# One LayerNorm statistics group instead of two, and another TensorE mark, at the entry of the first FFN

## The chip, the cores and the metric

One Trainium2 chip with 8 cores. Each core runs the same program on its own sequence (batch 8, one sequence of 2048 x 1024 for each core); no core waits for another. The time is in device microseconds of the slowest core.

## The reference

Four sublayers, each behind a LayerNorm and with a residual: a Mamba block, a gated FFN, causal attention, and the same FFN again.

```python
x = x + mamba(layernorm(x), W_in, conv_w, W_x, W_dt, b_dt, W_Bp, D_param, W_out)
x = x + ffn(layernorm(x), w_gate, w_up, w_down)
x = x + attn(layernorm(x), W)
x = x + ffn(layernorm(x), w_gate, w_up, w_down)

def ffn(x, w_gate, w_up, w_down):        # weights are int32 of -127..127
    gate = x @ (w_gate / 127).T          # 1024 -> 3072
    up   = x @ (w_up   / 127).T
    return (silu(gate) * up) @ (w_down / 127).T
```

## The kernel before

The instructions of each engine stand in the order in which the program text issues them (`em.op`); waits are on counting semaphores, and a mark such as `s_pe.mark()` is the count that a semaphore has reached at that point of the text.

**Mamba** works through the 2048 rows in 8 chunks of 256 (k = 0 to 7), each in 8 pairs. In the last chunk the FFN's gate weights are loaded beside it as int32 on SP's DMA queue and cast to bf16 by GpSimd, 16 units of 128 x 1536 (`emit_w_unit`, L803 to L826; SyncE issues the load, GpSimd casts, three staging slots in turn). `mamba_tail(7)` ends the block: VectorE adds the first half (L751), TensorE does 32 matmuls (L764), whose end is the mark `mk_t1[7]`, which is also `mk_mamba_pe_end`; VectorE waits for it and adds the second half (L774, `mk_mamba_ve_end`), and ScalarE's queue writes the sum to DRAM. GpSimd's last Mamba operation is `mk_mamba_gp_end`.

**The first FFN** (`ffn`, L871) has 4 chunks of 512 rows. Its first chunk finds its four input tiles in SBUF already, preloaded by `emit_ffn1_preamble`. `f_ln_tiles(c, tts, col0)` normalises some of them: `ln_stats_group` (L263) squares each tile on ScalarE (L269), sums it on VectorE (L278), does three small VectorE operations (L282, L284, L286), one square root on ScalarE (L291) and two or three small ones on VectorE. Then, tile by tile, VectorE normalises (L311), TensorE transposes 8 blocks (L322) and VectorE evacuates (L332). The first normalisation waits for a list of marks (L926 to L928).

What follows in the text, for the first FFN alone: 16 more units of `emit_w_unit`, which load and cast the up weights; then, on **ScalarE's queue**, 8 DMAs that write the cast gate weights to a bf16 copy in DRAM (`wg_c`, 768 KB each) and 8 that do so with the up weights (`wu_c`), each waiting for its casts (L952 to L960). The copies are read again by the last FFN. Then the first chunk's gate phase: 24 blocks of 8 matmuls (L993) into two PSUM banks in turn, each followed by a Silu on ScalarE (L1003), which frees the bank; then 24 blocks with the up weights, then the down projection (L1097). As the Silus stand behind the 16 cache DMAs in ScalarE's order, the first of them can't start before the last of those DMAs has been issued.

Of the kernel before, what the change touches and what calls it, by code (L numbers as in the profile page):

```python
# [26 lines left out]
NKM = L // TCM  # L27
# [130 lines left out]
def build_nc():  # L158
# [29 lines left out]
    with ExitStack() as ctx:  # L188
# [60 lines left out]
        s_pe = Sem(ctx.enter_context(nc.semaphore("s_pe")))  # L249
# [139 lines left out]
        def mamba_transpose(k, mk_free):  # L389
            par = k % 2  # L390
            banks = [4, 5]
            for tt in range(NTM):
                mk_tr = transpose_tile(xnbf[tt][:], banks[tt],
                                       mk_ln[k][tt], mk_free[tt])
                trdone[("m", tt)] = mk_tr
                mk_xnt[k] = evac_xnt(xnt[par], 256, tt, banks[tt], mk_tr)
# [183 lines left out]
        def phaseA_z_pair(kk, zp):  # L580
            par = kk % 2
            bkx = zp % 2
            for half in range(2):
                ci = NCI + 2 * zp + half
                wait_mm = [mk_xnt[kk], xzbank[bkx] if half == 0 else None]
                for dj in range(ND):
                    em.op("tensor",
                          lambda e, dj=dj, ci=ci, bkx=bkx, half=half, par=par: e.matmul(  # L588
                              psb[bkx][:, half * TCM:(half + 1) * TCM],
                              win_bf[:, dj * 4096 + ci * P: dj * 4096 + (ci + 1) * P],  # L590
                              xnt[par][:, dj * 256:(dj + 1) * 256],
                              start=(dj == 0), stop=(dj == ND - 1)),
                          wait=(wait_mm if dj == 0 else ()),
                          inc=([(s_pe, 1)] if (dj == ND - 1 and half == 1) else ()))
            mk_mm = s_pe.mark()
            w_sil = [mk_mm]
            if kk >= 1:
                w_sil.append(mk_gp_hist.get((kk - 1, zp)))
            elif zp == 0:
                w_sil.append(mk_startup)  # L600
            em.op("scalar",
                  lambda e, zp=zp, bkx=bkx: e.activation(
                      sz_bf[:, 2 * zp * TCM: 2 * (zp + 1) * TCM],
                      psb[bkx], AF.Silu),
                  wait=w_sil, inc=[(s_se, 1)], drain=False)
            xzbank[bkx] = mk_sz[(kk, zp)] = s_se.mark()
# [32 lines left out]
        def wout_t0(k, pi):  # L639
            w0 = [mk_gp_hist[(k, pi)]]  # L640
            if pi == 0:
                w0.append(mk_c67[0])
            for j in range(2):
                ci = 2 * pi + j
                for half in range(2):
                    em.op("tensor",
                          lambda e, ci=ci, half=half, bk=6 + half: e.matmul(  # L647
                              psb[bk],
                              y_bf[:, ci * TCM: ci * TCM + P],
                              wout_bf[:, ci * 1024 + half * 512: ci * 1024 + (half + 1) * 512],  # L650
                              start=(ci == 0), stop=(ci == NCI - 1)),
                          wait=(w0 if (j == 0 and half == 0) else ()),
                          inc=([(s_pe, 1)] if (j == 1 and half == 1) else ()))
# [149 lines left out]
        def emit_w_unit(gi):  # L803
            m2, r = divmod(gi, 16)
            dj, hh = divmod(r, 2)
            slot = (r % 2) if m2 == 0 else (r % 3)
            srcw = wg_t if m2 == 0 else wu_t
            dstw = wg_bf_g if m2 == 0 else wu_bf_g
            w = [mk_xz_last]
            if slot == 2:  # L810
                w.append(mk_mamba_pe_end)
            if w_prev[slot]:
                w.append(w_prev[slot])
            mkd = dma("sync", wstg[slot][:],
                      srcw[dj * P:(dj + 1) * P, hh * 1536:(hh + 1) * 1536],
                      wsem[slot], wait=w)
            cw = [mkd]
            if m2 == 1 and r == 0:
                cw += [mk_mamba_pe_end, mk_mamba_ve_end, mk_mamba_sta,
                       mk_mamba_stb]  # L820
            em.op("gpsimd",
                  lambda e, dj=dj, hh=hh, dstw=dstw, slot=slot: e.tensor_copy(
                      dstw[:, dj * H + hh * 1536: dj * H + (hh + 1) * 1536],
                      wstg[slot][:]),
                  wait=cw, inc=[(s_gp, 1)], drain=False)
            w_prev[slot] = w_mk[gi] = s_gp.mark()  # L826
# [17 lines left out]
        for k in range(NKM):  # L844
            for pi in range(8):
                phaseB_pair(k, pi)
                if k + 1 < NKM:
                    phaseA_xc_pair(k + 1, pi)
                    phaseA_z_pair(k + 1, pi)
                if k == NKM - 1 and N_SUBLAYERS >= 2:  # L850
                    emit_w_unit(2 * pi)
                    emit_w_unit(2 * pi + 1)
            if k + 1 == NKM - 1:
                mk_xz_last = s_pe.mark()
            wout_t0(k, 7)
            mamba_tail(k)
            if k + 1 < NKM:
                xp_sec(k + 1)
                if k + 2 < NKM:
                    mamba_load_ln(k + 2)  # L860
                    mamba_transpose(k + 2, [mk_xpe_k[k + 1], mk_xpe_k[k + 1]])
            if k == NKM - 2 and N_SUBLAYERS >= 2:
                ffn1_pre.update(emit_ffn1_preamble())

        mk_mamba_pe_end = s_pe.mark()
        mk_mamba_ve_end = s_ve.mark()
        mk_mamba_gp_end = s_gp.mark()
# [3 lines left out]
        def ffn(src, dst, first, region, store_mark_fn, pre=None):  # L871
# [6 lines left out]
            def fxt(c, tt):  # L878
                if pre and c == 0 and tt >= 2:
                    return fxB[tt - 2]  # L880
                if c % 2 == 1 and tt < 2:
                    return fxB[tt]
                return fxA[tt]
# [15 lines left out]
            def f_ln_tiles(c, tts, col0):  # L899
                tiles = [fxt(c, tt) for tt in tts]  # L900
                if pre and c == 0:
                    mk_x = pre["mk_loads"]
                else:
                    for i, tt in enumerate(tts):
                        gtile = c * NTF + tt
                        w = list(store_mark_fn(gtile))
                        if tt < 2:
                            if c <= 1:
                                w += region["xin"]
                            else:  # L910
                                w.append(mk_fst_chunk[c - 2])
                            if first and c == 1:
                                w.append(mk_fst_chunk[0])
                        else:
                            if c == 0:
                                w += region["xin"]
                            else:
                                w.append(mk_fst_chunk[c - 1])
                        mk_x = dma("scalar", tiles[i][:],
                                   src[gtile * P:(gtile + 1) * P, :],  # L920
                                   sd_x[c % 2], wait=w)
                mst = ln_stats_group([t[:] for t in tiles], col0, [mk_x])
                for i, tt in enumerate(tts):
                    col = col0 + i
                    ew = trdone.get(("f", tt % 2))
                    if pre and c == 0 and i == 0 and tts[0] == 0:  # L926
                        ew = [mk_mamba_pe_end, mk_mamba_gp_end,
                              mk_mamba_ve_end, ew]  # L928
                    mkn = ln_norm(fxn[tt % 2][:], tiles[i][:], col, mst,
                                  ew, first=(i == 0))  # L930
                    bank = 4 + tt % 2
                    mk_tr = transpose_tile(fxn[tt % 2][:], bank, mkn,
                                           tr_banks[bank])
                    trdone[("f", tt % 2)] = mk_tr
                    tr_banks[bank] = evac_xnt(fxnt[c % 2], 512, tt, bank,
                                              mk_tr)
                mk_xnt_f[c] = tr_banks[4 + tts[-1] % 2]

            f_ln_tiles(0, [0, 1], 8)
            f_ln_tiles(0, [2, 3], 10)  # L940

            mk_wg = [None] * ND
            mk_wu = [None] * ND
# [31 lines left out]
            for c in range(NKF):  # L975
# [72 lines left out]
                if c + 1 < NKF and not (first and c == 0):  # L1048
                    f_ln_tiles(c + 1, [0, 1], 8)
# [93 lines left out]
        if N_SUBLAYERS >= 2:  # L1143
# [13 lines left out]
                              pre=ffn1_pre)  # L1157
# [349 lines left out]
```

How the kernel before makes its waits and increments, by code:

```python
        def run(e, fn=fn, waits=waits, incs=incs, nd=need_drain):  # L141
            if nd:
                e.drain()
            for h, v in waits:
                e.wait_ge(h, v)
            r = fn(e)
            for h, d in incs:
                r = r.then_inc(h, d)
```

## Time and profile before

| | |
|---|---|
| median of 2 runs | 3245.6 us (3245.02 to 3246.18) |
| the profiled execution | 3245.18 us |
| its span, slowest core (core 2) | 3243.6 us |
| spans of the other cores | 3218.1 to 3240.8 us |
| granted TensorE clock, all cores | 0.799 to 0.804 of full |
| busy share of the span | TensorE 61%, VectorE 30%, ScalarE 22%, GpSimd 11% |
| DMA | 233 MB, mean 72 GB/s over the span |

The profile is of one execution. The span goes from the first to the last instruction of a core; the time of the execution is 1.6 us longer. Busy shares are means over very different stages: the passage from Mamba to the first FFN, which the change touches, is some 60 us long (1240 to 1300 us on the slowest core) and TensorE does almost nothing in it. The timelines below are in microseconds from the start of the span of the core named. In them q1 is the DMA queue of the weight loads (SyncE issues them) and q10 that of ScalarE.

### The profile page before, as it was taken

To read this page: it belongs to the slowest core of one execution; us is meant where nothing else is said; L and a number is where in the kernel's file an instruction comes from. 1 tells how busy PE (TensorE), PEld (TensorE's weight loads), DVE (VectorE), ACT (ScalarE), POOL (GpSimd) and SP (SyncE) were. 2 spreads that over 40 slices of the span, in tenths; PEclk is the share of its full clock that TensorE was granted. 3 is DMA by queue.
4 is the path that set the end of the run, shared out by engine and by line. 5 is a ranking of instruction groups with operands and counts; after the bars stand their busy time and mean duration, and the time that the engine had idled before them with its cause. 6 is when DMAs were issued, how large, how long until landed. Compare 5 with 4: busy or idle time off the path is not lost.

```text
span 3243.6 us, 29776 instructions; the slowest of 8 cores (3218.1 to 3243.6 us)
## 1 busy us (share of the span) xinstructions
PE 1965.5 (61%) x9274; PEld 966.6 (30%) x9432; DVE 966.0 (30%) x1617; ACT 729.7 (22%) x1164; POOL 363.2 (11%) x420
## 2 busy tenths in 40 slices
PE   0365455555555542954868668216986686768597
PEld 0243333333333321421323233112443332324242
DVE  3234444444344452102202121353432122212121
ACT  0244445454454530101101010110010201101010
POOL 0212222222222243031000000000000000000000
PEclk9667676767767665987988889658998798889899
DMA  7200000000000058243030211442133312030303
GB/s 241 91 14 17 11 27 1 27 1 26 27 1 27 1 175 280 84 153 117 14 115 3 72 58 46 137 157 79 40 110 104 146 46 72 30 101 13 117 1 101
DMA packets 69852, 233.32 MB, mean 72 GB/s; under 512 B 8450, under 2 KB 8578, under 8 KB 67652
## 3 DMA queue, kind: packets, MB, share of 16 engines
q10 hardware_dynamic: 38016, 124.80, 11.3%
q1 hardware_dynamic: 27460, 91.92, 9.0%
q0 software_dynamic: 4224, 14.68, 1.2%
q8 instruction: 82, 1.34, 0.2%
q14 instruction: 70, 0.57, 0.1%
HBM read 170.55 MB, written 60.82 MB: 71 GB/s over the span
## 4 chain that ended last, share of the span: by engine, by line
PE 38%; DMA 21%; DVE 12%; issue 8%; ACT 8%; DVEq 4%; POOL 3%; POOLq 3%; ACTq 2%; SPq 0%
PE ps_s L1027 16%; DMA arena<-wd_c 7%; PE ps_s L993 5%; DVEq L143 4%; DMA arena<-xs 3%; PE ps_s L1097 3%; PE ps L1097 3%; POOLq L143 3%; ACT L683 2%; POOL arena L564 2%; PE ps_s L1350 2%; DVE arena L520 2%; PE ps L764 2%; PE ps_s L1276 2%; PE ps L322 2%
## 5 line engine op out<-in xcount | busy, mean ns | idle before, releaser
L1027 PE MATMUL ps_s<-arena 128*128 128x512 bf16 x2256 | 506.2, 385 | 10.8 <-DVE arena L332 8.6
L588 PE MATMUL ps_s<-arena 128*128 128x256 bf16 x1024 | 208.0, 389 | 350.4 <-ACT arena L512 347.9
L322 PE MATMUL ps<-arena 128*128 128x128 bf16 x512 | 63.5, 307 | 474.7 <-DVE arena L311 474.7
L1027 PEld LDWEIGHTS ps_s<-arena 128*128 128x128 bf16 x2304 | 227.9, 99 | 287.8 <-issue 24.6
L1097 PE MATMUL ps_s<-arena 128*128 128x512 bf16 x752 | 209.2, 398 | 144.2 <-DMA arena<-wd_c 95.4
L269 ACT ACTIVATE arena<-arena 128x1024 bf16<-128x1024 f32 x64 | 67.6, 1056 | 893.7 <-DMA arena<-xs 791.2
L588 PEld LDWEIGHTS ps_s<-arena 128*128 128x128 bf16 x1024 | 134.1, 135 | 417.6 <-issue 366.9
L503 PE MATMUL ps_s<-arena 128*128 128x256 bf16 x1024 | 168.0, 334 | 114.7 <-DVE arena L451 64.8
L1042 DVE TENSOR_TENSOR arena<-arena,ps_s 128x512 bf16<-128x512 f32 x144 | 99.0, 688 | 422.1 <-ACT arena L1036 422.1
L1097 PE MATMUL ps<-arena 128*128 128x512 bf16 x752 | 210.8, 401 | 0.9
L322 PEld LDWEIGHTS ps<-arena 128*128 128x128 bf16 x512 | 50.2, 139 | 491.0 <-issue 491.0
L993 PE MATMUL ps_s<-arena 128*128 128x512 bf16 x752 | 172.6, 390 | 39.0 <-ACT arena L1003 35.5
L1113 DVE SCALAR_TENSOR_TENSOR arena<-ps_s,arena 128x512 f32<-128x512 f32 x32 | 19.9, 683 | 522.4 <-PE ps L1097 522.4
L1036 ACT ACTIVATE arena<-ps_s 128x512 f32<-128x512 f32 x144 | 86.0, 597 | 386.6 <-PE ps_s L1027 386.5
L503 PEld LDWEIGHTS ps_s<-arena 128*128 128x128 bf16 x1024 | 121.4, 119 | 170.0 <-issue 129.8
L574 ACT ACT_TABLE_LOAD x57 | 73.1, 1283 | 405.0 <-POOL arena L564 398.1
L701 DVE TENSOR_SCALAR arena<-arena 128x512 f32<-128x512 f32 x64 | 28.6, 447 | 415.7 <-ACT arena L688 415.7
L1097 PEld LDWEIGHTS ps_s<-arena 128*128 128x128 bf16 x768 | 66.0, 100 | 281.1 <-issue 238.7
L278 DVE TENSOR_REDUCE arena<-arena 128x1 f32<-128x1024 f32 x64 | 75.0, 1214 | 173.3 <-DMA arena<-xs 137.3
L993 PEld LDWEIGHTS ps_s<-arena 128*128 128x128 bf16 x768 | 76.6, 100 | 134.4 <-issue 48.9
L647 PE MATMUL ps<-arena 128*128 128x512 bf16 x226 | 81.9, 492 | 54.8 <-POOL arena L739 49.7
L1097 PEld LDWEIGHTS ps<-arena 128*128 128x128 bf16 x768 | 78.5, 102 | 102.7 <-issue 21.2
(91 smaller groups left out, 2343.6 us busy)
## 6 DMA issues: line engine op xcount, KB each, us to landing
xs<-arena ACTq DMA_DIRECT2D x48, 512.0 KB, 2.9
arena<-xs ACTq DMA_DIRECT2D x48, 512.0 KB, 4.6
arena<-wd_c SPq DMA_DIRECT2D x84, 256.0 KB, 2.6
arena<-wd_c ACTq DMA_DIRECT2D x84, 256.0 KB, 2.7
arena<-wg_t SPq DMA_DIRECT2D x16, 768.0 KB, 4.9
arena<-wu_t SPq DMA_DIRECT2D x16, 768.0 KB, 9.4
arena<-x ACTq DMA_DIRECT2D x16, 512.0 KB, 3.9
arena<-w_in ACTq DMA_DIRECT2D x8, 1024.0 KB, 10.9
```

Of the source, the lines that this page charges most:

```text
L143: e.drain()
L278: lambda e, s=t, j=col0 + i: e.reduce_sum(g_nsum[:, j:j + 1], s, axis=AX.X, negate=True),
L322: lambda e, s=xn_bf_tile, dj=dj, pbf=pbf: e.transpose(pbf[:, dj * P:(dj + 1) * P], s[:, dj * P:(dj + 1) * P], g_ident),
L503: lambda e, dj=dj, ci=ci, bkx=bkx, half=half, par=par: e.matmul(psb[bkx][:, half * TCM:(half + 1) * TCM], win_bf[:, dj * 4096 + ci * P: dj ...
L574: lambda e, p=p, pp=pp: e.activation(u_bf[:, 2 * p * TCM: 2 * (p + 1) * TCM], r2_p[pp][:], AF.Silu),
L588: lambda e, dj=dj, ci=ci, bkx=bkx, half=half, par=par: e.matmul(psb[bkx][:, half * TCM:(half + 1) * TCM], win_bf[:, dj * 4096 + ci * P: dj ...
L647: lambda e, ci=ci, half=half, bk=6 + half: e.matmul(psb[bk], y_bf[:, ci * TCM: ci * TCM + P], wout_bf[:, ci * 1024 + half * 512: ci * 1024 ...
L993: lambda e, hi=hi, dj=dj, bk=bk, par=par, wsrc=wsrc: e.matmul(psb[bk], wsrc[:, dj * H + hi * P: dj * H + (hi + 1) * P], fxnt[par][:, dj * ...
L1027: lambda e, hi=hi, dj=dj, bk=bk, par=par, wsrc=wsrc: e.matmul(psb[bk], wsrc[:, dj * H + hi * P: dj * H + (hi + 1) * P], fxnt[par][:, dj * ...
L1036: lambda e, hi=hi, bk=bks[0]: e.activation(gs[hi % 2][:], psb[bk], AF.Silu, scale=1.0 / 127.0),
L1042: lambda e, hi=hi, bk=bks[1]: e.tensor_mul(h_sb[:, hi * 512:(hi + 1) * 512], gs[hi % 2][:], psb[bk]),
L1097: lambda e, hi=hi, tt=tt, half=half, bk=bk, slot=slot: e.matmul(psb[bk], h_sb[:, hi * 512 + tt * P: hi * 512 + (tt + 1) * P], wd_sb[slot][ ...
```

## The change

A new mark `mk_b7_pe` is taken in the last Mamba chunk, before the last pair's output matmuls (`wout_t0(7, 7)`) and before `mamba_tail(7)`. The first normalisation of the first FFN waits for it in place of `mk_mamba_pe_end`; it goes on waiting for the marks of GpSimd and VectorE. And in the first FFN, first chunk, one call of `f_ln_tiles` with four tiles takes the place of two calls with two. The second FFN, which has no preamble, keeps its two calls. `ln_stats_group` then issues four squares and four sums, and each small operation and the root once, over four columns.

```diff
@@ the last Mamba chunk, after its eighth pair
+            if k == NKM - 1:
+                mk_b7_pe = s_pe.mark()
             wout_t0(k, 7)
             mamba_tail(k)
@@ f_ln_tiles
                     if pre and c == 0 and i == 0 and tts[0] == 0:
-                        ew = [mk_mamba_pe_end, mk_mamba_gp_end,
+                        ew = [mk_b7_pe, mk_mamba_gp_end,
                               mk_mamba_ve_end, ew]
@@ ffn
-            f_ln_tiles(0, [0, 1], 8)
-            f_ln_tiles(0, [2, 3], 10)
+            if pre:
+                f_ln_tiles(0, [0, 1, 2, 3], 8)
+            else:
+                f_ln_tiles(0, [0, 1], 8)
+                f_ln_tiles(0, [2, 3], 10)
```

## Rows read from the trace of the kernel before

**Rows 1.** Spans of the cores: the slowest core and its mean clock.
```profile
core 2: 3243.6 us, clock 0.802
```

**Rows 2.** Chain that ended last, core 2, 1285 to 1312 us: start, duration, what.
```profile
1285.54 12.20 DMA arena<-wu_t
1297.86 1.47 POOL arena L822
...
1301.25 0.60 ACT arena L1003
1301.99 9.77 PE ps_s L993 x34
```

**Rows 3.** Timeline of ScalarE and its queue, core 2: start, duration, instruction [idle before].
```profile
1238.14 1.28 ACT L291 ACT_TABLE_LOAD   x1 [0.40 <-DVE arena L286]
...
1240.83 1.06 ACT L269 ACTIVATE arena<-arena 128x1024 bf16<-128x1024 f32 x1
...
1253.18 0.30 ACT L291 ACTIVATE arena<-arena 128x2 f32<-128x2 f32 x1 [11.20 <-DVE arena L286]
1253.26 5.25 ACTq L956 DMA_DIRECT2D wg_c<-arena  x8
1258.60 41.17 ACTq L956 DMA_DIRECT2D wu_c<-arena  x8
```

**Rows 4.** Timeline of VectorE, core 2, last Mamba additions to last evacuation.
```profile
1233.58 1.28 DVE L774 TENSOR_TENSOR arena<-arena,ps 128x512 f32<-128x512 f32 x2 [8.97 <-PE ps L764]
1234.78 2.34 DVE L278 TENSOR_REDUCE arena<-arena 128x1 f32<-128x1024 f32 x2
...
1237.84 0.16 DVE L286 SCALAR_TENSOR_TENSOR arena<-arena 128x2 f32<-128x2 f32 x1 [0.23 <-ACT arena L269]
...
1250.08 1.12 DVE L282 TENSOR_SCALAR arena<-arena 128x2 f32<-128x2 f32 x1
...
1251.59 1.44 DVE L286 SCALAR_TENSOR_TENSOR arena<-arena 128x2 f32<-128x2 f32 x1 [0.15 <-issue]
...
1259.19 0.69 DVE L332 COPY arena<-ps 128x1024 bf16<-128x1024 bf16 x1 [1.37 <-PE ps L322]
```

**Rows 5.** Timeline of TensorE, core 2: the first gate matmuls.
```profile
1260.51 5.96 PE L993 MATMUL ps_s<-arena 128*128 128x512 bf16 x15 [1.43 <-POOL arena L822]
```

**Rows 6.** Timeline of GpSimd, core 2: the first three up-weight casts.
```profile
1239.69 4.74 POOL L822 CAST arena<-arena 128x1536 bf16<-128x1536 int32 x3 [14.26 <-DMA xs<-arena]
```

**Rows 7.** DMA queues of core 2, 1247 to 1258 us: packets, MB, share of engines.
```profile
q1 hardware_dynamic: 570, 3.12, 88.7%
```

**Rows 8.** DMA queues of core 2, 1258 to 1288 us.
```profile
q1 hardware_dynamic: 880, 4.80, 57.6%
q10 hardware_dynamic: 920, 5.08, 40.7%
```

**Rows 9.** Timelines of core 0: first and last up-weight cast, then the cache writes.
```profile
1234.82 5.02 POOL L822 CAST arena<-arena 128x1536 bf16<-128x1536 int32 x3 [16.27 <-DMA xs<-arena]
...
1293.89 1.46 POOL L822 CAST arena<-arena 128x1536 bf16<-128x1536 int32 x1 [2.76 <-DMA arena<-wu_t]
...
1243.76 4.86 ACTq L956 DMA_DIRECT2D wg_c<-arena  x8
```

**Rows 10.** Timelines of core 1: first and last up-weight cast, then the cache writes.
```profile
1244.44 4.76 POOL L822 CAST arena<-arena 128x1536 bf16<-128x1536 int32 x3 [17.52 <-DMA xs<-arena]
...
1305.24 1.46 POOL L822 CAST arena<-arena 128x1536 bf16<-128x1536 int32 x1 [1.71 <-DMA arena<-wu_t]
...
1253.12 5.44 ACTq L956 DMA_DIRECT2D wg_c<-arena  x8
```

**Rows 11.** Timelines of core 5: first and last up-weight cast, then the cache writes.
```profile
1235.33 4.74 POOL L822 CAST arena<-arena 128x1536 bf16<-128x1536 int32 x3 [14.70 <-DMA xs<-arena]
...
1291.44 1.46 POOL L822 CAST arena<-arena 128x1536 bf16<-128x1536 int32 x1 [2.74 <-DMA arena<-wu_t]
...
1248.73 5.05 ACTq L956 DMA_DIRECT2D wg_c<-arena  x8
```

## The prediction

> **What bounds the kernel now.** I read the spans of the cores first: core 2 ends last, with 3243.6 us [rows 1], and the sum below is made on it. Then I read the chain that ended last, around the place of the change, 1230 to 1310 us. It does not go through the LayerNorm of the first FFN. It goes through the load of the last up weights, their cast on GpSimd at 1297.86, a Silu on ScalarE at 1301.25, and only then through gate matmuls, from 1301.99 on [rows 2]. The timeline of ScalarE and its queue shows why: the eight `wg_c` writes are issued from 1253.26, straight behind the square root of the second statistics group (1253.18), and the issue of the eight `wu_c` writes fills 1258.60 to 1299.77, because each waits for its casts [rows 3]. All Silus stand behind them. The timeline of TensorE has the other side: the normalised input is complete at 1259.88 [rows 4], the first gate matmuls run at 1260.51, 15 of them are recorded (two blocks of 8, as many as there are banks), and they end at 1266.47 [rows 5]. TensorE then stands until 1301.99, 35.5 us. So the LayerNorm is early by 35 us, and what sets the end is when the sixteenth up-weight unit is loaded and cast.
>
> **The new mark.** It costs and brings nothing. The first normalisation stands in VectorE's own order behind the two additions of L774, which waited 8.97 us for the last Mamba matmul [rows 4]; what is queued behind them on VectorE can't run before that matmul, with whatever mark. The same holds for the wait on `mk_mamba_ve_end`, which stays.
>
> **The merged group.** It removes one set of five small VectorE operations and one root with its round trip, and it puts the sums of tiles 2 and 3 ahead of tile 0's normalisation. The last evacuation comes earlier. From the second root (1253.18) to the end of the last evacuation (1259.88) two tiles take 6.7 us [rows 3, 4]; four take no more than 13.4, and with the one root at about 1243 (below) the input is complete at about 1256.4 or before, 3.5 us earlier. The cover of this gain is the 35.5 us stall of TensorE: worth nothing while that stands, and about 3.5 us if it were gone.
>
> **What the merged group moves.** The only root, and with it everything behind the second root on ScalarE: the eight `wg_c` writes. When does the root end now? The sums start at 1234.78 and four take 2 x 2.34 us, to 1239.46. Of the squares, the fourth starts at 1240.83 today, behind a table load (1.28) and a root (0.30) that will now come later; without these it is read out at about 1240.4. Then L286 (0.16), a gap of 0.14, the table load and the root: 1242.3 [rows 3, 4]. That is the early end. The late end: from 1239.69 GpSimd casts three units back to back until 1244.43 [rows 6], and beside casts the small operations are slow: L282 to L286 took 2.95 us from 1250.08 to 1253.03, L286 alone 1.44 instead of 0.16 [rows 4]. From 1239.5 this gives L286's end at 1242.5 and the root's at 1244.3. I take the middle, 1243.3, as only a part of the three meets a cast. The writes are thus issued 10.0 us earlier than at 1253.26 (9.0 to 11.0). Each DMA is the same; only its time moves. The next thing on the same queue, the `wu_c` writes, still waits for the casts, so ScalarE is not set free earlier.
>
> The page SBUF — State Buffer of the Trainium skill (Who interferes with whom) has VectorE and GpSimd take an exclusive lock on a port pair for whole instructions. By that rule each of the three small operations could wait for a whole cast of about 1.5 us, the root would come near 1245, and the cost below would be some 1.3 us smaller; the measured 2.95 us for the three is milder.
>
> **What the earlier writes cost.** The up-weight loads on q1 have the DMA engines to themselves until the writes of q10 start to move. From 1247 to 1258 q1 moved 3.12 MB, 0.284 MB/us [rows 7], although the writes had been issued from 1253.26; their bytes begin some 4.5 us after the issue. From 1258 to 1288 q1 moved 4.80 MB, 0.160 MB/us, and q10 5.08 MB [rows 8]: the engines are full, 57.6% and 40.7%, and the loads get half of the bytes. Bringing the writes forward by 10.0 us turns 10.0 us at 0.284 into 10.0 us at 0.160, so 1.24 MB of the loads are still to do; at 0.160 MB/us these take 7.7 us. The last cast, the issue of the last `wu_c` write, the first Silu and the restart of TensorE follow one another as now, so all move by 7.7 us.
>
> The page DMA: Bandwidth & Descriptors of the Trainium skill (Queues, rings and completion order) says that each DMA engine goes round robin between the queues that have work, packet by packet. The packets of 1258 to 1288, 880 against 920 [rows 8], agree. Taken strictly, half of the 0.329 MB/us of both queues is 0.165 and the delay is 7.2 us. It is the rule that speaks against this change.
>
> The eight cores are an experiment on the same thing, since their second root comes at different times after the first up-weight cast. Core 0: writes 8.94 us after it, last cast 59.07 us after it [rows 9]. Core 1: 8.68 and 60.80 [rows 10]. Core 5: 13.40 and 56.11 [rows 11]. Core 2: 13.57 and 58.17 [rows 2, 3, 6]. Mean of cores 0 and 1 against mean of cores 5 and 2: writes 4.7 us earlier, last cast 2.8 us later, 0.6 us for each. Rates gave 0.77 for each. The steepest pair (1 against 5) gives 0.99, the flattest (0 against 2) 0.19. For the shift of 9 to 11 us the bounds are then 1.7 and 10.9 us. I keep 7.7, from the rates of core 2 itself, as that is the slowest core.
>
> **Sum.** Mark 0, input earlier 0 (hidden), up-weight casts +7.7, behind them nothing that catches up: after 1301.99 gate and up phase run on TensorE, one block behind the other. On core 2's span 3243.6 + 7.7 = 3251.3. The profiled execution took 3245.2 us, 1.6 more than its span and 0.4 less than the median of 3245.6; so 3252.9 us.
>
> **Rivals.**
> 1. *No change.* The loads lose less than the rates say, because they alternate between bursts and waits for a slot, and the writes fit in between. For it: cores 0 and 2 differ by only 0.9 us, and q1 used only 88.7% of the engines from 1247 to 1258 [rows 7]. Against it: the bytes of rows 8. It gives 1.7 us or less: 3245 to 3247.
> 2. *Faster: the write queue runs dry.* The `wg_c` writes come forward into time in which the engines were idle (11.3% of 11 us, 1.2 us), and if q10 is empty before the last load, the last loads run alone. Price: at most the 1.2 us, 3244. It decides if q10 has moved all it can be given by then. At 0.169 MB/us [rows 8] the 6.3 MB of `wg_c` last 37 us from about 1248, until 1285; by then about 11 of 16 units are cast and five `wu_c` writes (3.9 MB) wait, enough for 23 us, to 1308, while the last cast is due at 1305.6. So it holds only if q10 is about 20% faster than it is.
> 3. *Faster: the input sets the gate phase after all.* Then about 3.5 us are won: 3242. Against it are the 35.5 us of stall. This would need the casts to be done before 1257.
> 4. *The cost at its upper bound*, 10.9 us, by cores 1 and 5, or more if the other cores' writes, which all come earlier too, slow the loads in addition: 3256 to 3260.
>
> **How the numbers follow.** Forecast (3247 to 3257): 0.68. Rival 1: 0.18. Rival 2: 0.05. Rival 3: 0.03. Rival 4 beyond 3257: 0.06. The range reaches from rival 2's 3244 to 3258, the upper bound with the 1.2 us between two executions of the kernel before; it leaves out rival 3 and the end of rival 4. A change of 2% is 65 us, about what a measurement of this kernel can tell from no change; no case comes near it, and only something unseen, such as TensorE's clock in the long later stages, could. At the restart that clock costs nothing new: TensorE has stood still before the restart in both cases. Faster by over 2% 0.01, within 2% 0.97, slower 0.02.
>
> **What would show each step.** In the changed kernel's timeline on core 2: four sums in a row on VectorE, one root at 1242 to 1244.5 if Mamba ends at the same time; `wg_c` writes 3 to 5 us after the first up-weight cast instead of 13.6; the first gate matmul near 1256, and a TensorE stall of 46 us or so behind it; q10 moving bytes from about 1248, q1 near 0.16 MB/us from then on; the last cast 64 to 67 us after the first instead of 58.2. The mark's step is wrong if the first normalisation starts before the additions of L774 have ended. The cost's step is wrong if the last cast stays at 58 us with the writes at 3 to 5. The whole is wrong if TensorE's stall is gone.

## The result, and the profile after

| | before | after |
|---|---|---|
| median of all runs | 3249.15 us (29 runs) | 3263.6 us (30 runs) |
| median of the runs that the ratio counts | 3244.8 us (16 runs) | 3256.4 us (18 runs) |
| ratio after/before, 95% interval | | 1.0042 (1.0026 to 1.0057) |
| profiled execution: time, span | 3245.18, 3243.6 us | 3255.09, 3253.5 us |
| first to last up-weight cast, mean of the 8 cores | 58.3 us | 67.4 us |
| input of the FFN complete behind the first up-weight cast, mean of the 8 cores | 18.7 us | 15.5 us |

The change makes the kernel slower, by 0.42%: 13.6 us of 3249, between 8.4 and 18.5. In both programs some executions are lengthened on one die by a lower clock, whatever the kernel; the medians of all runs hold these too, the second line of medians and the ratio leave them out.

The rows that answer to those of before. The slowest core is now core 6; core 2 is shown because the forecast was made on it (spans of the cores):

```profile
core 2: 3250.1 us, clock 0.796
...
core 6: 3253.5 us, clock 0.796
```

The chain that ended last still goes through the up-weight loads and casts into the first Silu. Timeline of ScalarE and its queue, core 2, beside [rows 3]:

```profile
1246.55 1.06 ACT L269 ACTIVATE arena<-arena 128x1024 bf16<-128x1024 f32 x1
...
1250.22 1.28 ACT L291 ACT_TABLE_LOAD   x1 [2.52 <-DVE arena L286]
1250.33 1.52 ACTq L961 DMA_DIRECT2D wg_c<-arena  x3
1251.51 0.30 ACT L291 ACTIVATE arena<-arena 128x4 f32<-128x4 f32 x1
1251.93 3.94 ACTq L961 DMA_DIRECT2D wg_c<-arena  x5
1255.96 58.58 ACTq L961 DMA_DIRECT2D wu_c<-arena  x8
1314.74 1.28 ACT L1008 ACT_TABLE_LOAD   x1 [62.93 <-POOL arena L822]
```

One root instead of two. The issue of the `wg_c` writes begins at 1250.33, even before the root they stand behind (1251.51), during its table load; the `wu_c` writes now fill 58.6 us instead of 41.2. Timeline of VectorE, core 2, beside [rows 4]:

```profile
1241.11 1.28 DVE L774 TENSOR_TENSOR arena<-arena,ps 128x512 f32<-128x512 f32 x2 [8.98 <-PE ps L764]
1242.31 4.59 DVE L278 TENSOR_REDUCE arena<-arena 128x1 f32<-128x1024 f32 x4
...
1247.24 1.44 DVE L284 TENSOR_TENSOR arena<-arena 128x4 f32<-128x4 f32 x1
1248.82 1.26 DVE L286 SCALAR_TENSOR_TENSOR arena<-arena 128x4 f32<-128x4 f32 x1
...
1263.29 0.69 DVE L332 COPY arena<-ps 128x1024 bf16<-128x1024 bf16 x1 [1.37 <-PE ps L322]
```

The four sums are behind the additions of L774, new mark or not. Two of the three small operations run into casts (1.44 and 1.26 us instead of 0.16). They are not slow in general: every small VectorE operation of this LayerNorm that took over 0.3 us, on all cores of all eleven profiled executions of this document, ended within 0.03 us of the end of a cast. It waits until the running cast is over. The input is complete at 1263.98. Timelines of GpSimd and of TensorE, core 2, beside [rows 6] and [rows 5]:

```profile
1247.20 4.28 POOL L822 CAST arena<-arena 128x1536 bf16<-128x1536 int32 x3 [14.09 <-DMA xs<-arena]
...
1312.64 1.46 POOL L822 CAST arena<-arena 128x1536 bf16<-128x1536 int32 x1 [3.22 <-DMA arena<-wu_t]
```

```profile
1264.62 5.96 PE L998 MATMUL ps_s<-arena 128*128 128x512 bf16 x15 [1.43 <-DVE arena L332]
1316.77 8.49 PE L998 MATMUL ps_s<-arena 128*128 128x512 bf16 x29 [46.19 <-ACT arena L1008]
```

From the first up-weight cast (1247.20) the input is complete after 16.8 us, before it was 20.2: 3.4 us won, and lost at once, since TensorE now stands for 46.2 us instead of 35.5. The last cast starts 65.4 us after the first, before 58.2. DMA queues of core 2, 1255 to 1300 us, beside [rows 8] (packets, MB, share of the engines):

```profile
q1 hardware_dynamic: 1373, 7.51, 57.2%
q10 hardware_dynamic: 1399, 7.66, 42.1%
```

Loads (q1) and writes (q10) get equal parts, 0.167 and 0.170 MB/us, from 8 us after the first cast on, where before the loads were alone on this core until 18 us after it.

### The profile page after: what moved, and what is told of

Same layout as the page of the kernel before. It is cut to its first block, busy times and chain, and to the rows that moved or that the text cites. A ratio compares the mean times of both kernels' runs of the same rounds, so it can differ in the third digit from the quotient of the medians.

```text
span 3253.5 us, 29917 instructions; the slowest of 8 cores (3224.8 to 3253.5 us)
## 1 busy us (share of the span) xinstructions
PE 1995.6 (61%) x9432; PEld 972.7 (30%) x9432; DVE 963.1 (30%) x1612; ACT 729.5 (22%) x1163; POOL 362.2 (11%) x420
## 4 chain that ended last, share of the span: by engine, by line
PE 39%; DMA 20%; DVE 13%; ACT 9%; issue 8%; DVEq 4%; POOLq 3%; POOL 3%; ACTq 2%; SPq 0%
PE ps_s L1032 16%; DMA arena<-wd_c 7%; PE ps_s L998 5%; DVEq L143 4%; DMA arena<-xs 3%; PE ps_s L1102 3%; PE ps L1102 3%; POOLq L143 3%; ACT L683 2%; POOL arena L564 2%; PE ps_s L1355 2%; DVE arena L520 2%; DMA arena<-wu_t 2%; PE ps L764 2%; PE ps_s L1281 2%
## 5 line engine op out<-in xcount | busy, mean ns | idle before, releaser
L588 PE MATMUL ps_s<-arena 128*128 128x256 bf16 x1024 | 214.4, 398 | 341.5 <-ACT arena L512 339.2
L322 PE MATMUL ps<-arena 128*128 128x128 bf16 x512 | 63.4, 306 | 475.2 <-DVE arena L311 475.2
L503 PE MATMUL ps_s<-arena 128*128 128x256 bf16 x1024 | 170.8, 339 | 110.9 <-DVE arena L451 62.6
L1102 PE MATMUL ps<-arena 128*128 128x512 bf16 x768 | 212.9, 401 | 0.0
L647 PE MATMUL ps<-arena 128*128 128x512 bf16 x256 | 92.9, 501 | 41.6 <-POOL arena L739 41.4
```

What stands on the lines that cost most here:

```text
L322: lambda e, s=xn_bf_tile, dj=dj, pbf=pbf: e.transpose(pbf[:, dj * P:(dj + 1) * P], s[:, dj * P:(dj + 1) * P], g_ident),
L647: lambda e, ci=ci, half=half, bk=6 + half: e.matmul(psb[bk], y_bf[:, ci * TCM: ci * TCM + P], wout_bf[:, ci * 1024 + half * 512: ci * 1024 ...
L1102: lambda e, hi=hi, tt=tt, half=half, bk=bk, slot=slot: e.matmul(psb[bk], h_sb[:, hi * 512 + tt * P: hi * 512 + (tt + 1) * P], wd_sb[slot][ ...
```

## The experiments

The quantity that decides can be read on every core of every profiled execution: the start of the last up-weight cast less the start of the first, here called the stretch. All figures in this table but the ratio are means over the 8 cores of one profiled execution, worked out from the timelines of GpSimd, ScalarE and TensorE. "Rest" is the span less the time of the first up-weight cast: all that comes behind Mamba. How far two executions of the same work differ in it can be read from the kernel before and the one with the mark alone: 2.9 us in the rest, 0.5 us in the stretch.

| kernel | `wg_c` writes issued behind first cast | stretch | TensorE restarts behind first cast | rest | ratio to before (95%) |
|---|---|---|---|---|---|
| before | 11.4 | 58.3 | 62.4 | 1993.1 | 1 |
| changed | 1.1 | 67.4 | 71.5 | 2002.9 | 1.0042 (1.0026 to 1.0057) |
| changed, again | 1.7 | 67.2 | 71.4 | 2004.0 | 1.0033 (1.0008 to 1.0058) |
| mark alone | 11.7 | 57.8 | 61.9 | 1996.0 | 1.0003 (0.9983 to 1.0023) |
| merged, writes held to the sixth cast | 12.9 | 56.4 | 60.6 | 1992.8 | 0.9987 (0.9966 to 1.0008) |
| merged, writes held to the third cast | 4.4 | 63.5 | 67.7 | 1998.0 | not given (2 runs) |
| two groups, writes early | -2.5 | 65.7 | 69.9 | 2000.5 | 1.0021 (1.0000 to 1.0042) |
| merged, `wu_c` writes first | 53.0 | 51.0 | 64.4 | 1995.4 | 1.0013 (0.9983 to 1.0042) |
| merged, writes behind the gate phase | 62.3 | 37.6 | no stall | 1954.8 | 0.9872 (0.9829 to 0.9916) |
| two groups, writes behind the gate phase | 63.3 | 37.9 | no stall | 1955.2 | 0.9895 (0.9824 to 0.9966) |
| merged, writes issued by SyncE | behind the loads | 38.4 | no stall | 1952.8 | 0.9884 (0.9853 to 0.9915) |

The theory (W): the merged group moves the `wg_c` writes ahead, and these take the DMA engines from the up-weight loads, behind whose casts every Silu stands. The rival (L): a second source, in the merged group itself or in the mark, since 1.0042 is more than the 1.0024 of the forecast.

### The changed kernel again, and the mark alone

> The changed kernel once more, beside the variants. Theory W (the wg_c writes, moved ahead, halve the bandwidth of the up-weight loads): the stretch from the first to the last up-weight cast is 64 to 69 us on every core (before: 56.1 to 60.8), the time 8 to 10 us over before, ratio 1.0025 to 1.003. Rival L (the measured 1.0042 has a second source in the merged group or in the mark, besides the writes): ratio 1.004 or more with the same stretch.

Measured: ratio 1.0033, stretch 65.5 to 68.7 us on the eight cores. The ratio lies between what W gave (up to 1.003) and what L gave (1.004 or more). Its interval, 2.6 to 18.9 us, holds the 9 us of W, and 1.0042 too, so this run does not decide between them.

```diff
-                        ew = [mk_mamba_pe_end, mk_mamba_gp_end,
+                        ew = [mk_b7_pe, mk_mamba_gp_end,
                               mk_mamba_ve_end, ew]
```

> The kernel before with the new TensorE mark alone, two statistics groups. Theory W: no change, ratio 1.000, stretch of the up-weight casts 56 to 61 us, first normalisation still behind the additions of L774. Rival L: if the mark is a part of the cost, ratio 1.001 or more.

Measured: 1.0003, stretch 57.8 on the mean (55.7 to 61.6 on the cores). The mark does nothing that these runs can tell, as its place in VectorE's order said.

### The merged group with the writes held back

```diff
-                              wait=[mkk[dj]], inc=[(sd_cache, 16)],
+                              wait=[mkk[dj], w_mk[21]], inc=[(sd_cache, 16)],
```

> The changed kernel with one added wait: the wg_c writes wait for the sixth up-weight cast, about where they stood in the kernel before. Theory W: the loss is gone, stretch 57 to 60 us, ratio 1.000 within 0.001, though the normalised input is still ready 3 to 4 us earlier. Rival L: ratio stays 1.003 to 1.004, since the merged group is untouched.

Measured: 0.9987, stretch 56.4, a little under the 57 to 60 expected. On its slowest core, core 7, the root is where the merged group puts it, and the writes are issued 8.7 us after its start (timeline of ScalarE, then of GpSimd):

```profile
1250.22 0.30 ACT L291 ACTIVATE arena<-arena 128x4 f32<-128x4 f32 x1
1258.96 5.63 ACTq L961 DMA_DIRECT2D wg_c<-arena  x8
```

```profile
1245.91 4.27 POOL L822 CAST arena<-arena 128x1536 bf16<-128x1536 int32 x3 [16.17 <-DMA xs<-arena]
...
1302.15 1.46 POOL L822 CAST arena<-arena 128x1536 bf16<-128x1536 int32 x1 [2.39 <-DMA arena<-wu_t]
```

The stretch is 56.2 us there. The merged group is all in, the input is complete 16.7 us behind the first cast (mean; 2.1 us earlier than before, not the 3 to 4 expected), and the whole loss is gone. This is against L: the interval ends at 1.0008.

### The writes moved ahead without the change

```diff
             f_ln_tiles(0, [0, 1], 8)
+            if first:
+                for dj in range(ND):
+                    em.op("scalar", lambda e, dj=dj: e.dma_start(
+                              wg_c[dj * P:(dj + 1) * P, :],
+                              wg_bf[:, dj * H:(dj + 1) * H]),
+                          wait=[w_mk[2 * dj + 1]], inc=[(sd_cache, 16)],
+                          drain=False)
             f_ln_tiles(0, [2, 3], 10)
...
-                for dstw, cache, mkk in ((wg_bf, wg_c, mk_wg),
-                                         (wu_bf, wu_c, mk_wu)):
+                for dstw, cache, mkk in ((wu_bf, wu_c, mk_wu),):
```

> The kernel before, two groups and old mark, but the eight wg_c writes stand between the first and the second group in ScalarE's order, so they are issued right behind the first square root. Theory W: the whole loss without the change, writes about 1 us after the first up-weight cast, stretch 64 to 69 us, ratio 1.0025 to 1.004. Rival L: ratio 1.000, stretch 56 to 61 us.

Measured: 1.0021, stretch 65.7. The writes came 2.5 us ahead of the first cast, not 1 us behind it as expected. The interval of the time reaches down to no change; the stretch leaves no doubt, it lies between 63.4 and 67.9 us on all eight cores, where before it was 56.1 to 60.8. The timelines of its slowest core, core 0, ScalarE and then GpSimd:

```profile
1241.48 1.80 ACTq L943 DMA_DIRECT2D wg_c<-arena  x3
...
1243.37 4.99 ACTq L943 DMA_DIRECT2D wg_c<-arena  x5
...
1253.11 0.30 ACT L291 ACTIVATE arena<-arena 128x2 f32<-128x2 f32 x1 [2.29 <-DVE arena L286]
```

```profile
1244.53 4.74 POOL L822 CAST arena<-arena 128x1536 bf16<-128x1536 int32 x3 [16.81 <-DMA xs<-arena]
...
1308.84 1.46 POOL L822 CAST arena<-arena 128x1536 bf16<-128x1536 int32 x1 [0.52 <-DMA arena<-wu_t]
```

Two roots, the second 8.6 us behind the first cast (this core before: writes straight behind that root, at 8.9), and yet 64.3 us. So moving the writes alone brings the cost, and holding them back takes it away. What they do in the first 8 us behind the first up-weight cast is in the DMA queues of this core, 1244.53 to 1252.53 us:

```profile
q10 hardware_dynamic: 328, 1.78, 103.9%
```

That is the only data queue with packets in the window (a packet's whole time counts where it starts, so the share can pass 100%): the loads that were issued as soon as the casts freed their slots, from 1246.07 on, moved nothing for over 6 us.

### How much each microsecond costs

```diff
-                              wait=[mkk[dj]], inc=[(sd_cache, 16)],
+                              wait=[mkk[dj], w_mk[18]], inc=[(sd_cache, 16)],
```

> The changed kernel with the wg_c writes waiting for the third up-weight cast, so that they are issued about 4.3 us after the first cast, between the changed kernel (1.1 to 1.7) and the held one (12.9). Theory W1 (each us that the writes come forward costs the same): on the line through 12.9 us / 56.4 us and 1.4 us / 67.3 us, stretch 64.6 us. Theory W2 (the first microseconds behind the first cast cost most, because then the loads have nothing in flight and the writes fill the engines alone): less than the line says, stretch 61 to 63.5 us.

Measured: 63.5 us, 62.4 to 65.9 on the cores, at the edge of what W2 gave and 1.1 us under the line. From 12.9 to 4.4 us each microsecond cost 0.83, from 4.4 to the changed kernel's 1.4 it cost 1.27. This leans to W2, but with a standard deviation of about 1.2 us from core to core in one execution it does not settle the curve by itself. Earlier still it stops: at -2.5 us the stretch is 65.7, 1.6 us shorter. The reason is in the DMA queues: writes so early have moved most of what they can before the end, and the write queue then waits for casts. Core 0 of that run, 50 to 60 us behind the first cast, and core 6 of the changed kernel in the same stretch:

```profile
q1 hardware_dynamic: 374, 2.05, 63.2%
q10 hardware_dynamic: 230, 1.26, 30.1%
```

```profile
q1 hardware_dynamic: 290, 1.60, 58.3%
q10 hardware_dynamic: 305, 1.67, 40.9%
```

On the mean of the cores the loads move 2.03 MB in these 10 us and the writes 1.02, in the changed kernel 1.74 and 1.57. This is rival 2 of the prediction, seen where the writes are still earlier than in the changed kernel.

### The order of the two sets of writes

```diff
-                for dstw, cache, mkk in ((wg_bf, wg_c, mk_wg),
-                                         (wu_bf, wu_c, mk_wu)):
+                for dstw, cache, mkk in ((wu_bf, wu_c, mk_wu),
+                                         (wg_bf, wg_c, mk_wg)):
```

> The changed kernel with the order of the two sets of cache writes swapped: the wu_c writes first, each when its casts are done, the wg_c writes behind the last cast. During the loads the write queue then only gets one write of 768 KB for two loads. Theory W (the loads get what the write queue leaves, half if it never runs dry): two thirds of 0.33 MB/us is 0.22 MB/us, stretch about 50 us (48 to 53), the first Silu after eight more issues of 0.4 to 0.6 us each, so 3 to 6 us faster than before, ratio 0.998 to 0.999. Rival S (loads are slowed by the mere presence of writes, not by their amount): stretch 60 us or more, ratio 1.001 or more.

The stretch came out within what W gave, 51.0 us. DMA queues of the slowest core, core 4, 1266 to 1296 us:

```profile
q1 hardware_dynamic: 1196, 6.49, 68.1%
q10 hardware_dynamic: 646, 3.58, 28.5%
```

With one write for two loads the loads get 0.216 MB/us. It is the amount of writes beside them that counts, against rival S. But the time did not fall (1.0013, 0.998 to 0.999 expected), and the expectation had that wrong. Timeline of ScalarE, core 4:

```profile
1249.45 49.76 ACTq L961 DMA_DIRECT2D wu_c<-arena  x8
1299.30 8.70 ACTq L961 DMA_DIRECT2D wg_c<-arena  x8
1308.20 1.28 ACT L1008 ACT_TABLE_LOAD   x1 [58.49 <-issue]
```

The eight `wg_c` writes, all ready, take 8.7 us to issue (8.7 to 9.4 on the cores), where eight of 0.4 to 0.6 us were expected, 3.2 to 4.8 in all, and then comes a table load. From the last cast to TensorE's restart it is 13.4 us on the mean, before it was 4.1: 7.3 us won in the stretch, 9.2 lost behind it.

### The cover taken away

All sixteen writes go to ScalarE's queue behind the gate phase's Silus; once from the changed kernel, once from the kernel before:

```diff
                     for phase in range(2):
+                        if first and phase == 1:
+                            for dstw, cache, mkk in ((wg_bf, wg_c, mk_wg),
+                                                     (wu_bf, wu_c, mk_wu)):
+                                for dj in range(ND):
+                                    em.op("scalar", lambda e, dj=dj, dstw=dstw, cache=cache: e.dma_start(
+                                              cache[dj * P:(dj + 1) * P, :],
+                                              dstw[:, dj * H:(dj + 1) * H]),
+                                          wait=[mkk[dj]], inc=[(sd_cache, 16)],
+                                          drain=False)
                         mkw = mk_wg if phase == 0 else mk_wu
```

> The changed kernel with all sixteen cache writes issued from ScalarE's order behind the gate phase's Silus, ahead of the up phase. Loads have the DMA engines to themselves and the Silus wait for no cast. Theory W with the cover taken away: stretch 39 to 42 us, gate phase starts at about 1256 on a core like core 2 of before and runs through without the stall of 35 to 46 us, about 42 us faster than before, ratio 0.987. Rival C (the stall is given back: the up phase waits for casts or the writes slow the first down-projection loads): ratio 0.992 or more.

> The kernel before (two groups, old mark) with the same late cache writes. Theory W: as with the merged group, but the gate phase starts 3 to 4 us later, since now the LayerNorm is on the path: ratio 0.988, 3.5 us over the merged one, which is what the merged group is worth without its cover. Rival: the start of the gate phase isn't on the path there either (the up casts set the up phase): both the same.

Measured: 0.9872 and 0.9895, stretches 37.6 and 37.9. Timeline of TensorE on the slowest core of the first, core 3, then what TensorE waited for most from 1235 to 1480 us (total, times, longest), and the gate and up phases of the second on its slowest core, core 0:

```profile
1270.11 5.28 PE L999 MATMUL ps_s<-arena 128*128 128x512 bf16 x16 [1.05 <-DVE arena L332]
1275.89 79.59 PE L999 MATMUL ps_s<-arena 128*128 128x512 bf16 x368 [0.50 <-ACT arena L1009]
1356.64 1.67 PE L1103 MATMUL ps_s<-arena 128*128 128x512 bf16 x4 [1.16 <-DVE arena L1017]
```

```profile
PE ps_s L1103 <- POOL arena L1078: 40.9, 21, 3.6
```

```profile
1259.44 85.59 PE L994 MATMUL ps_s<-arena 128*128 128x512 bf16 x384 [1.05 <-DVE arena L332]
```

The two phases run through, from 1270.11 to the down projection at 1356.64; the longest waits of the down projection are what they were (40.9 us; before, on core 2 and up to 1510 us, 40.7), so little is given back, against rival C. The gate phase starts 18.3 us behind the first cast with the merged group and 19.3 us with the two groups: 1.0 us, not the 3.5 expected. On the cores the start varies from 16.6 or 16.7 to 21.3 us in both, so this 1.0 us can't be told from nothing. The rest differs by 0.4 us, and the times can't tell the two apart. A part of the missing gain is in the small VectorE operations, which meet casts: in the changed kernel the five of them took 2.0 us together (mean), here 3.4, against 3.6 for the ten of the two groups.

```diff
-                        em.op("scalar",
+                        em.op("sync",
                               lambda e, dj=dj, dstw=dstw, cache=cache: e.dma_start(
```

> The changed kernel with the sixteen cache writes issued by SyncE, behind its up-weight loads, instead of by ScalarE. The loads are alone on the engines until their last issue, and no Silu stands behind a write. As with the late writes: stretch 37 to 40 us, gate phase runs through from about 16 us after the first cast, ratio 0.985 to 0.988. If the writes, which now start some 30 us earlier than in the late variant and stand ahead of the first down-projection loads in the same queue, disturb the up phase or those loads, ratio above 0.989.

Measured: 0.9884, stretch 38.4. Timeline of SyncE's queue on the slowest core, core 1, and the gate and up phases there:

```profile
1240.32 40.80 SPq L259 DMA_DIRECT2D arena<-wu_t  x14
1281.22 6.21 SPq L961 DMA_DIRECT2D wg_c<-arena  x8
1287.53 12.44 SPq L961 DMA_DIRECT2D wu_c<-arena  x8
```

```profile
1263.71 85.57 PE L998 MATMUL ps_s<-arena 128*128 128x512 bf16 x384 [1.05 <-DVE arena L332]
```

The sixteen writes are issued from 1281.22 on, in the middle of the gate phase, and all 384 matmuls of both phases run without a gap. Rest and ratio are those of the late variants within what these runs can tell. Any of the three beats the kernel before by some 1.1 to 1.3%, though the intervals reach from 0.3 to 1.8%.

## Why the prediction was right or wrong

**Right.** The place and the direction. The LayerNorm was covered, the gain in it (3.4 us on core 2, 3.3 on the mean, 3.5 forecast) came and was hidden; the mark was worth nothing; loads and writes shared the engines evenly. For core 2, on which the sum was made, the forecast held in its main parts: writes 3.1 us behind the first cast (3 to 5 forecast), TensorE's stall grown from 35.5 to 46.2 us (46), stretch 65.4 (64 to 67), and so 7.3 us longer, 7.7 forecast (8.5 in the repeat, so the closeness is in part luck). Rivals 1, 2 and 3 did not come.

**Right with some luck: the shift.** 10.0 us were forecast for it, and it was 10.4 on core 2, 11.4 - 1.1 = 10.3 on the mean. Counted from the start of the sums (1234.78 before, 1242.31 now), the one root started at 9.2 us where the middle of the forecast has 8.2. But the writes did not wait for it: their issue began at 8.0, where the forecast has 8.5, behind the root's end. The two errors go against each other. The small operations were not slowed in general, as "milder" has it, but each waited for the end of the cast it met, and on the cores none, one or two of the three did.

**Wrong: the price, taken from one core for the whole chip.** The step that failed is "I keep 7.7, from the rates of core 2 itself". The forecast was 7.7 us, the measurement 13.6 with 8.4 as its lower end. Of this the runs explain 9 to 10: the mean stretch grew by 9.1 us, that of core 6, which ends last now, by 9.9, and the rest by 9.8 (10.8 in the repeat; 6.9 and 8.0 if measured against the execution with the mark alone). The shift was as forecast, so the mis-sized term is the price of a microsecond by which the writes come forward: 0.77 in the sum, 9.1 / 10.3 = 0.88 on the mean, and from 0.5 to 1.1 on the single cores of this one pair of executions. In bytes: 30 us behind the first cast the loads of core 2 were 1.26 MB behind those of the kernel before, where the forecast had 1.24, but those of the mean of the cores 1.63 MB. Of the two rates in the price, the one shared with the writes was right (0.160 forecast; in the changed kernel 0.176 from 8 to 18 us behind the first cast, 0.159 from 20 to 50, mean). The one for loads alone, 0.284, is of one core in one stretch; with the writes out of the way the mean of the cores was 0.31 (from 8 to 18 us, writes late). On core 2 of the merged variant with late writes, the same 10 us:

```profile
q1 hardware_dynamic: 602, 3.31, 93.0%
```

An estimate with 0.31 alone and 0.16 to 0.18 shared gives a price of 0.7 to 0.9. That this is the whole reason for 0.88 is not shown. Rival 4 had a price of 0.99 and a cost of 10.9 us.

**Who is first does not explain it.** DMA queues of core 7 in the 8 us behind the first up-weight cast, in the kernel before:

```profile
q1 hardware_dynamic: 277, 1.55, 65.4%
```

and in the changed kernel:

```profile
q10 hardware_dynamic: 294, 1.61, 72.0%
q1 hardware_dynamic: 66, 0.41, 16.7%
```

In these 8 us the loads did not fall from 0.19 to 0.16 MB/us but to 0.05. At the first cast all three slots are full and no load is in flight; here the writes are issued 0.3 us after it, their bytes move first, and the first bytes of the loads come at 6.3 us instead of 2.5. It looks like the missing part of the price, and it happens on cores 1, 4, 5 and 7. On cores 0, 2, 3 and 6, core 6 among them, the loads' bytes are first as before, 2.5 us behind the first cast. DMA queues of core 6 in the changed kernel, the same 8 us:

```profile
q1 hardware_dynamic: 163, 0.90, 47.7%
q10 hardware_dynamic: 116, 0.70, 21.8%
```

Yet the price is the same in both groups: 9.9 us for 11.1 us of shift (0.89) where the writes are first, 8.2 us for 9.5 (0.87) where the loads are. And from the sixth to the third cast, with the loads first on all cores, it was 0.83. What the writes win by being first was not seen in the stretch.

**Wrong, but of no effect here: the gain without its cover.** The prediction had 3.5 us for the merged group if the stall were gone. With the stall gone it was 1.0 us, inside the spread of the cores.

**The level.** The sum stood on 3245.2 us, and that was right: the median that goes with the ratio is 3244.8 in the kernel before. In the changed kernel it is 3256.4, inside the range of 3244 to 3258 and 3.5 us above the forecast of 3252.9; the ratio on the base of the sum gives 3258.8, just outside. The median of all runs, 3263.6, is far outside, and nothing in the sum answers to the 7.2 us between the two medians.

**Left open.** The measured 1.0042 and 1.0033 are 13.6 and 10.7 us, the medians that go with the first are 11.6 us apart, and 9 to 10 is inside both intervals. No run showed a second source: mark alone 1.0003, merged with held writes 0.9987. Whether the few microseconds beyond are noise can't be told by these runs. In the profiled pair itself the spans grew by 13.3 us on the mean, and 3.5 of these lie ahead of the first up-weight cast, where the kernels do the same work.

## What to carry to other kernels

An instruction that is taken away moves everything that stands behind it in its engine's order, and that includes the DMAs it issues. Before merging or advancing work that is already early, look at what is queued behind it and which transfers it will meet. Where eight cores are at hand, take the price of a term from all of them, and not from the one that happens to end last in one execution. A background write has no claim to a place in the queue of the engine whose next operation frees the bottleneck: here moving sixteen writes elsewhere was worth 1.2%, while the LayerNorm in front of them was worth nothing.

## What the runs showed of the hardware

- Two DMA queues with work share the engines evenly (7.51 and 7.66 MB in 45 us), but one that starts beside a busy one waits. Writes issued beside running loads moved their first bytes 3.7 to 4.9 us after the issue on seven of the eight cores of the kernel before (1.2 on the eighth), with idle engines after 0.8 us (writes late); loads issued behind eight queued writes moved nothing for over 6 us.
- Issuing eight DMAs of 768 KB on ScalarE took 5.25 us beside running loads (core 2 before), 8.7 us behind the `wu_c` writes, and 8.3 us with both queues empty before them (writes late, core 0). So it is not the fill of the write queue that decides; what does stays open.
- DMAs behind a root on ScalarE's queue were issued 1.2 us before the root ran, during the table load.
- The loads alone moved 0.31 MB/us (mean of the eight cores, 8 to 18 us behind the first cast, writes late), both queues together 0.33: one queue nearly fills the engines.
- A small VectorE operation that meets a cast on GpSimd waits for its end: up to 1.48 us instead of 0.16 to 0.18, and the end within 0.03 us of the cast's end each time, in eleven profiled executions.
